# Attention mask added on VectorE, maximum subtracted on GpSimd, later slots for P.V and the value product, feed-forward weights loaded one by one

## The reference, cut to what matters

```python
for i in range(6):                                  # DEPTH
    x = attn_layer(shift_tokens(x), Wqkv[i], q_scale[i], k_scale[i], Wo[i]) + x
    x = ffn_layer(shift_tokens(x), ln_g[i], ln_b[i], W1[i], b1[i], W2[i], b2[i]) + x

# attn_layer: 16 heads of 64, windows of 32 tokens, each looking at itself and the window before
q = rotary(l2norm(q) * qs); k = rotary(l2norm(k) * ksc)
sim = einsum('bhwie,bhwje->bhwij', bq, bk2) * 8.0
sim = where(mask, -finfo.max, sim); attn = softmax(sim, -1)
out = einsum('bhwij,bhwje->bhwie', attn, bv2)  @ Wo
# ffn_layer: layer norm, then (a * gelu(gate)) @ W2 + b2, with a, gate = split(xn @ W1 + b1)
# shift_tokens: the second half of the channels comes from the token before
```

## Time and profile before

| | us |
|---|---|
| three runs: median (lowest to highest) | 1740.41 (1739.14 to 1745.62) |
| the profiled execution | 1741.98 |
| its span, first to last instruction | 1740.2 |
| PE busy | 1666.1 (96%) |
| DVE busy | 1381.5 (79%) |
| POOL busy | 1187.3 (68%) |
| ACT busy | 1092.9 (63%) |
| share of PE in the chain that ended last | 89% |

### The profile page before, as it was taken

One profiled execution on the slowest core, in us unless ns is written; L12 is line 12 of the kernel. 1 busy time (PEld: TensorE's weight loads), 2 busy tenths in 40 slices (PEclk: granted clock), 3 DMA queues, 4 the chain that ended last, 5 costly groups with the idle time before them and its releaser, 6 DMA issues.

```text
span 1740.2 us, 74075 instructions
## 1 busy us (share of the span) xinstructions
PE 1666.1 (96%) x31420; PEld 1210.5 (70%) x31420; DVE 1381.5 (79%) x2661; ACT 1092.9 (63%) x1943; POOL 1187.3 (68%) x1163
## 2 busy tenths in 40 slices
PE   5889999999999999999999999999999999999995
PEld 2357777777777777677777677777677777677774
DVE  4688888887888888788888788888788887788863
ACT  2256666666666666566666566666666666566653
POOL 0377777776777767676776677677677777666751
PEclk9799999999999999999999999999999999999998
DMA  3032223332223323222323222333222332222222
GB/s 106 25 93 66 68 67 79 89 76 71 66 68 81 88 68 78 68 65 69 96 71 78 70 68 63 92 78 77 71 69 66 80 87 74 74 64 66 66 61 76
DMA packets 109735, 127.86 MB, mean 73 GB/s; under 512 B 52064, under 2 KB 55648, under 8 KB 109152
## 3 DMA queue, kind: packets, MB, share of 16 engines
q1 hardware_dynamic: 109408, 123.13, 27.9%
HBM read 20.27 MB, written 2.10 MB: 13 GB/s over the span
## 4 chain that ended last, share of the span: by engine, by line
PE 89%; DVE 4%; SPq 2%; ACT 2%; DMA 2%; issue 1%; POOL 0%; ACTq 0%; DVEq 0%; POOLq 0%
PE QKb L471 21%; PE O L594 11%; PE F L499 9%; PE VTb L512 9%; PE S L471 9%; PE S L529 8%; PE S L559 5%; PE F L616 4%; PE F L628 4%; PE F L629 3%; PE S L522 2%; SPq L397 1%; DVE t L823 1%; PE F L568 1%; DMA prm<-in_params 1%
## 5 line engine op out<-in xcount | busy, mean ns | idle before, releaser
L968 POOL TENSOR_TENSOR t<-t 128x512 f32<-128x512 f32 x384 | 488.7, 1273 | 306.6 <-DVE t L823 298.7
L823 DVE TENSOR_TENSOR t<-QKb,table 128x1024 f32<-128x1024 f32 x384 | 468.8, 1221 | 156.8 <-ACT sq L668 156.3
L962 POOL TENSOR_TENSOR t<-t,rn 128x512 f32<-128x512 f32 x384 | 400.5, 1043 | 136.0 <-DVE rn L863 136.0
L471 PE MATMUL QKb<-wq_sb,x_sh 128*128 128x512 f32 x768 | 426.3, 637 | 12.4 <-DVE t L823 11.7
L668 ACT ACTIVATE sq<-QKb 128x512 f32<-128x512 f32 x384 | 230.8, 601 | 321.7 <-PE QKb L471 314.7
L499 PEld LDWEIGHTS F<-wo_sb,OT 128*128 128x128 f32 x1536 | 202.9, 193 | 89.6 <-issue 88.7
L512 PEld LDWEIGHTS VTb<-cst,t 128*128 128x128 f32 x1536 | 186.6, 141 | 104.8 <-issue 94.0
L512 PE MATMUL VTb<-cst,t 128*128 128x128 f32 x1536 | 230.6, 273 | 0.6 <-POOL t L962 0.5
L594 PEld LDWEIGHTS O<-PT,V 64*64 64x64 f32 x12288 | 199.2, 135 | 42.7 <-issue 41.8
L876 DVE TENSOR_REDUCE ss<-sq 128x16 f32<-128x1024 f32 x192 | 224.4, 1169 | 0.0
L594 PE MATMUL O<-PT,V 64*64 64x32 f32 x12288 | 219.2, 221 | 0.9 <-DVE rn L863 0.5
(11 more groups left out here) (136 smaller groups left out, 2165.9 us busy)
## 6 DMA issues: line engine op xcount, KB each, us to landing
V<-v_tok SPq DMA_DIRECT2D x1440, 64.0 KB, 2.0
wq_sb<-in_wqkv SPq DMA_DIRECT2D x36, 256.0 KB, 3.7
wo_sb<-in_wo SPq DMA_DIRECT2D x6, 512.0 KB, 5.0
xs<-xm SPq DMA_DIRECT2D x48, 64.0 KB
xs<-xm SPq DMA_DIRECT2D x48, 63.5 KB
w_sb<-in_w SPq DMA_DIRECT2D x6, 341.0 KB, 3.3
w_sb<-in_w SPq DMA_DIRECT2D x6, 192.0 KB, 3.1
y_spill<-OT SPq DMA_DIRECT2D x1, 1024.0 KB, 4.1
```

Source lines behind the costliest of these rows:

```text
L471: return pe.matmul(out_, x_sh[:, pr, P * tile:P * (tile + 1)], wq_sb[:, col:col + 512], start=True, stop=True)
L823: dve.tensor_tensor(t12[:, v, :, :].rearrange("p c (h d) -> p c h d", h=8), QK_ps.rearrange("p (h d) -> p h d", h=8).unsqueeze(1) .to_broa ...
L962: pool.tensor_tensor(w, w, rn[:, vv // 4, 8 * (vv % 4):8 * (vv % 4 + 1)].unsqueeze(2) .to_broadcast([P, 8, DH]), ALU.mult).then_inc(qk_nor ...
L968: pool.tensor_tensor(w, w, t12[:, v, 1, :].rearrange("p (h c d) -> p h c d", h=8, c=2)[:, :, ::-1, :], ALU.add).then_inc(add_done, 1)
```

## The change

- **Mask.** The two mask matmuls of each quad go, with `ident_bf` and `mask_bf`. The score matmuls write their banks afresh. DVE adds the mask from `cst` while it moves the scores from `S2` to `E` (semaphore `mask_done`), and takes the maximum from `E`. PE's value projection and PT now wait for `mask_done` where they waited for `sub_done`.
- **Subtraction.** POOL subtracts the maximum, in place in `E`, in a slot of its own (`L_SUB`).
- **Lags.** V from 6 to 8; exponent from 12 to 13, normalisation from 13 to 14, PT from 14 to 16, PV from 16 to 18. In the feed-forward WO from 21 to 22, MID from 24 to 26, SH from 24 to 25, XT from 29 to 33, W1 from 32 to 34, the end from 37 to 38; ST and NM stay at 27. TX goes from slot 6 to slot 7. `Y_BACK`, the slot in which the recurrence's result is transposed back, goes from `STEPS * SLOTS + 19` to `+ 27`.
- **Order in a slot.** All four engines' steps are written in another order. Of the parts named above: PE transposes ahead of the projection; DVE has Newton, END, ST and MID ahead of `t12`; POOL has scale, subtraction, normalisation, NM, and `t12`'s add last.
- **Feed-forward weights.** W1, W2 and the parameters have a semaphore each. W1 is reloaded at slot 36, after the last W1 product of the layer before, W2 at slot 38, and `prm` has two buffers and is loaded at slot 2.

```diff
-L_V = 6
-L_S, L_EXP, L_NORM, L_PT, L_PV = 11, 12, 13, 14, 16
-
-F_WO, F_MID, F_SH, F_ST, F_NM, F_XT, F_AFF = 21, 24, 24, 27, 27, 29, 29
-F_W1, F_GEL, F_HID, F_W2, F_END = 32, 32, 33, 35, 37
-TX = 6
+L_V = 8
+L_S, L_SUB, L_EXP, L_NORM, L_PT, L_PV = 11, 12, 13, 14, 16, 18
+
+F_WO, F_MID, F_SH, F_ST, F_NM, F_XT, F_AFF = 22, 26, 25, 27, 27, 33, 33
+F_W1, F_GEL, F_HID, F_W2, F_END = 34, 34, 35, 37, 38
+TX = 7
...
-                if slot == F_END + 1:
-
-                    wait(sp, ff_final, l * B)
-                    sp.dma_start(w1_sb[:, :], w1[l]).then_inc(in_ffn, 16)
-                    sp.dma_start(w2_sb[:, :, :], w2[l])\
-                      .then_inc(in_ffn, 16)
-                    sp.dma_start(prm[:, :], params[l]).then_inc(in_ffn, 16)
+                if slot == 2:
+
+                    wait(sp, ff_final, (l - 1) * B)
+                    sp.dma_start(prm[:, l % 2, :], params[l]).then_inc(in_prm, 16)
+                if slot == F_HID + 1:
+
+                    wait(sp, w1_ready, l * B * NCH)
+                    sp.dma_start(w1_sb[:, :], w1[l]).then_inc(in_w1, 16)
+                if slot == F_W2 + 1:
+
+                    wait(sp, w2_ready, l * B)
+                    sp.dma_start(w2_sb[:, :, :], w2[l]).then_inc(in_w2, 16)
...
-                        for p in range(2):
-                            pe.matmul(S2[:, p, 0:4 * KEYS], ident_bf[:, :], mask_bf[:, :], start=True, stop=False,
-                                      skip_group_check=True)
...
-                                                   start=False, stop=ct == 3, skip_group_check=True)
...
+                                                   start=True, stop=True)
...
-                        dve.tensor_reduce(mv_, Sv, AX_X, ALU.max).then_inc(max_done, 1)
-                        wait(dve, max_done, a + 1)
-                        wait(dve, pt_ready, a - 3)
-                        if a == 0:
-                            wait(dve, yT_done, 4)
-                        dve.tensor_tensor(E[:, k, :].rearrange("p (c b k) -> p b c k", c=4, b=2), Sv,
-                                          mv_.unsqueeze(3).to_broadcast([P, 2, 4, KEYS]),
-                                          ALU.subtract).then_inc(sub_done, 1)
...
+                    f, pr = batch(s, par, v, F_ST)
+                    if f is not None:
+                        wait(dve, xs_moved, 48 * (f + 1))
...
+                    f, pr = batch(s, par, v, F_MID)
+                    if f is not None:
+                        wait(dve, wo_ready, f + 1)
...
+                        dve.tensor_tensor(Ek, Sv, cst[:, C_MASK:C_MASK + 4 * KEYS]
+                                          .rearrange("p (c k) -> p c k", k=KEYS).unsqueeze(1)
+                                          .to_broadcast([P, 2, 4, KEYS]), ALU.add).then_inc(mask_done, 1)
+                        wait(dve, mask_done, a + 1)
+                        wait(dve, sub_done, a - 3)
+                        dve.tensor_reduce(mx[:, k, :], E[:, k, :].rearrange("p (c k) -> p c k", k=KEYS), AX_X, ALU.max)\
+                           .then_inc(max_done, 1)
...
+                    a, k, st, pr = quad(s, par, v, L_SUB)
+                    if live(a, QUADS):
+                        wait(pool, max_done, a + 1)
+                        w = E[:, k, :].rearrange("p (c k) -> p c k", k=KEYS)
+                        pool.tensor_tensor(w, w, mx[:, k, :].unsqueeze(2).to_broadcast([P, 8, KEYS]),
+                                           ALU.subtract).then_inc(sub_done, 1)
```

More of the change, by code:

```diff
@@ L476, in step @@
                     g = s * SLOTS + v
+                    u, vv, st, pr = unit(s, par, v, L_TR)
+                    if live(u, UNITS):
+                        wait(pe, qk_norm, u + 1)
+                        wait(pe, tr_evac, u)
+                        for i in range(4):
+                            mm = pe.transpose(VT_ps[:, P * i:P * (i + 1)], t12[:, vv, 0, P * i:P * (i + 1)], ident)
+                        mm.then_inc(tr_ready, 1)
                     if live(g, UNITS):
@@ L505, in step @@
-                    recurrence(in_fill(s, v, 0))
-                    u, vv, st, pr = unit(s, par, v, L_TR)
-                    if live(u, UNITS):
-                        wait(pe, qk_norm, u + 1)
-                        wait(pe, tr_evac, u)
-                        for i in range(4):
-                            mm = pe.transpose(VT_ps[:, P * i:P * (i + 1)], t12[:, vv, 0, P * i:P * (i + 1)], ident)
-                        mm.then_inc(tr_ready, 1)
-                    a, k, st, pr = quad(s, par, v, L_S)
@@ new lines, in step @@
+                    a, k, st, pr = quad(s, par, v, L_PT)
+                    if live(a, QUADS):
+                        wait(pe, p_norm, a + 1)
+                        wait(pe, mask_done, s_units(s, v))
+                        wait(pe, pt_evac, a)
+                        for ct in range(4):
+                            mm = pe.transpose(PT_ps[:, P * ct:P * (ct + 1)], E[:, k, P * ct:P * (ct + 1)], ident)
+                        mm.then_inc(pt_ready, 1)
+                    a, k, st, pr = quad(s, par, v, L_S)
@@ L636, in _ @@
         def _(act):
-            act.wait_ge(set_dve, 4)
+            act.wait_ge(set_dve, 2)
             act.wait_ge(mv_done, TILES)
@@ new lines, in step @@
+                    u, vv, st, pr = unit(s, par, v, L_SS)
+                    if live(u, UNITS) and vv % 2 == 0:
+                        wait(dve, sq_done, u + 2)
+                        dve.tensor_reduce(ss[:, vv // 4, 8 * (vv % 4):8 * (vv % 4) + 16],
+                                          sq[:, vv % 4:vv % 4 + 2, :].rearrange("p a (h d) -> p (a h) d", h=8),
+                                          AX_X, ALU.add).then_inc(ss_done, 1)
+                    recurrence(in_fill(s, v, 0))
+                    a, k, st, pr = quad(s, par, v, L_EXP)
@@ new lines, in step @@
+                    if live(a, QUADS):
+                        wait(dve, exp_done, a + 1)
+                        dve.tensor_reduce(sm[:, k, :], E[:, k, :].rearrange("p (c k) -> p c k", k=KEYS), AX_X, ALU.add)\
+                           .then_inc(sum_done, 1)
+                        wait(dve, sum_done, a + 1)
+                        wait(dve, p_norm, a - 3)
+                        dve.reciprocal(rs[:, k, :], sm[:, k, :]).then_inc(rs_done, 1)
+                    recurrence(in_fill(s, v, 1))
```

286 lines of the change are left out of this document (131 added, 155 removed).

## The result

The changed kernel takes **1825.76 us** (median of 4 runs, 1823.79 to 1827.37), the kernel before 1740.86 in the same comparison (4 runs, 1739.14 to 1745.62). The ratio is 1.048, with a 95% interval of 1.046 to 1.051: 85 us slower. The forecast was 1795 with a range of 1744 to 1830, so the sign and the range held, and the loss is 1.6 times the one forecast.

A forecast was written before the change was run, and what follows sets the result against it. PE alone was taken to bound the kernel at 33.35 us per step. Steady steps +37.7, irregular rest +4, clock +10, start +2 and +3, end +3 and -5 gave +54.7 on 1741.98, forecast 1795, range 1744 to 1830.

The forecast's parts named there:

- PE's floor: PE's own work per step without waits on other engines: falls from 33.35 to 32.25 us.
- the floor's two parts: On PE per step: mask matmuls removed save 0.87 us, the new order of matmul groups saves 0.23.
- The boundaries: At layer boundaries PE's wait for the affine step goes with separate weight and parameter loads: 20.7 us saved over five steps.
- MID to ST: Move of shifted rows between MID and the statistics takes 6.3 us, so PE stalls 1.7 per step before Q(4).
- POOL's convoy: NM, waiting for ST, stands ahead of slot 3's add on POOL; PE's slot 6 transposes wait, 0.9 us more per step.
- The step and the clock: Steady step of 34.9 us, 43 steps giving +37.7; PE's clock falling in one step of six or seven, +10 in all.
- The start: First steps: step 3's stall +2 us and the recurrence's DVE additions behind t12 +3.
- The recurrence's places: In the recurrence's first ten slots both its DVE additions stand behind t12: +3 us, range 0 to 6.
- The end: Last batches meet the same wait, +3 us; five mask groups and PE's wait for the recurrence's result go, -5.
- The move is hidden: Rival: the moved rows land before DVE has done the gates, PE keeps its floor; 1670 us, chance 10%.
- Only DVE's wait counts: Rival: POOL catches up and no clock is lost, step 33.95, about 1744 us, no change; chance 12%.
- the clock falls in every step: Rival: each step's stall lowers PE's clock, adding 60 to 80 us, about 1865; chance 8%.

The follow-up runs named there:

- best: st31 with the block of inverse square roots moved behind the maximum, in slots 1 and 5; 1762.82 us, 1.014 of before.
- st29: Changed kernel with layer norm statistics and normalisation two slots later (F_ST = F_NM = 29 instead of 27); 1746.58 us, 1.004 of before.
- before_ff: Kernel before with only the changed kernel's separate loads of W1, W2 and the parameters, old order otherwise; 1720.34 us, 0.990 of before.
- split_rows: Changed kernel with the 127-row transfer cut into 112 and 15 rows, single-row transfer kept; 1718.79 us, 0.987 of before.
- nm31: Changed kernel with only the normalisation's lag moved, F_NM from 27 to 31, statistics left in place; 1793.62 us, 1.030 of before.
- st31: Changed kernel with layer norm statistics and normalisation four slots later (F_ST = F_NM = 31 instead of 27); 1704.85 us, 0.979 of before.
- st31_rec: st31 with the filter's recurrence put back on PE and DVE where the kernel before has it; 1703.08 us, 0.976 of before.
- split_no_row: Changed kernel with the 127-row transfer cut into 112 and 15 rows and the single-row transfer left out; 1704.35 us, 0.979 of before.

## Why the prediction was right in kind, and short in size

**PE's floor, right.** Slots without a wait are seen in the table: 4.70, 3.35, 5.58, 3.10, 3.81, 3.62 (best), 4.70, 3.45. Their sum is 32.3; the forecast was 32.25. The 0.1 between the forecast's 3.35 and the 3.45 of slot 7-0 stands in every kernel of the new order (st29 has 3.80) and is the one part missed. Only the sum of the floor's two parts is shown, 0.87 for the mask and 0.23 for the order: no run parts them in the new order.

**The boundaries, right, with a new item missed.** The wait for the affine step is gone, and before_ff shows the gain alone. But the steps that begin a layer take 36.2 to 38.4 in the changed kernel, not 35.2. Of this 0.68 is in 1-2, which is 4.03 there; the timeline of DVE has the item:

```profile
891.82 1.75 DVE L797 TENSOR_TENSOR table<-cst,scales 128x256 f32<-128x256 f32 x2
```

Two products for the rotary tables stand ahead of slot 0's. The old order absorbed them; the new one has no slack in this place. The rest is mostly in 3-4, which takes 5.2 to 6.2 in these steps: the residual sum ends 1.26 after Q(2) there and not 0.98, so the statistics and all behind them come later by as much. In two of the five steps the clock fell as well (below).

**MID to ST, right and a little small.** The step on which all rested, taking 6.3 from the last batch and not 2.0 from V's rows, held: 6.5. MID ends 0.98 after Q(2), forecast 1.02, and Q(4) came 10.51 after Q(2), where the forecast had 10.34. The reason for the 6.3 wasn't in the forecast; it is the 127 rows. The forecast had quoted the Trainium skill, "DMA: Bandwidth & Descriptors", section "Anatomy of one DMA — SWDGE (gpsimd) path", with a fixed 2.0 us and bytes over bandwidth, and set it aside for the row; that section is on DMAs issued by GpSimd, and these are issued by SP. Its rule fits the large transfers in split_rows, which land after 2.1, and not the 127 rows. The page's rule on the number of engines, which fits what was measured, was not looked at.

**POOL's convoy, right.** 0.9 per step, in the trace of after and by nm31.

**The step and the clock.** A step is 35.23, not 34.9: 0.15 of it in 3-4, 0.05 in 4-5 and 5-6, and 0.1 in 7-0. Over 43 steps that is **+14**. The clock was booked at 10, from an idle 1.58 that was followed by the lower level. PE's idle ahead of Q(4) is about as long as that, 1.42 to 1.63 in 36 of the 43 steps, and behind none of these did the clock fall. It fell to the lower level three times in the 43 steps: behind idles of 1.99 in step 8, 1.96 in step 16 and 2.52 in step 23, and not behind one of 2.02 in step 24. The waits in steps 8 and 24:

```profile
340.13 1.10 PE L475 MATMUL QKb<-wq_sb,x_sh 128*128 128x512 f32 x2 [1.99 <-DVE t L853]
...
909.94 1.10 PE L475 MATMUL QKb<-wq_sb,x_sh 128*128 128x512 f32 x2 [2.02 <-DVE t L853]
```

The windows of the changed kernel (stretch, us, busy us of each engine, granted clock, DMA), in step 8 up to and behind the wait, then a steady stretch:

```profile
335.00:340.00 5.00, 3.14 (x75) 1.80 (x73) 2.04 (x7) 4.00 (x7) 1.65 (x3) 1.00 0.30 73
340.00:350.00 10.00, 9.87 (x151) 6.49 (x152) 7.51 (x17) 4.43 (x8) 8.05 (x8) 0.66 0.35 94
...
1000.00:1100.00 100.00, 93.35 (x1786) 65.73 (x1785) 79.01 (x153) 62.55 (x112) 81.47 (x81) 1.00 0.28 69
```

The three steps with a fall are the longest, 38.4, 36.9 and 36.8, where boundary steps otherwise take 36.3 and other steps 35.2. So the falls cost at most some 4 together (an estimate from these lengths; step 23 has a late DMA issue in it too). So clock and irregular time together were 9 where 14 were booked, and the 43 steps: 51.7 forecast, plus 14, less 5 is the 61.0 measured.

**The start was mis-sized: +13.1, not +5.** The recurrence's places were booked at +3 and are worth 6 (st31 against st31_rec). The stall of step 3 was booked at the steady 2; that step took 36.1 against 30.9, and step 2 another 1.3. In step 3 PE has no W1 product yet (2-3 is 3.81, not 5.58), so it comes to the wait earlier and idles 3.5 in one piece, and the granted clock from 156 to 168 was 0.72: 3-4 takes 7.78.

**The end had the wrong sign: +11.3, not -2.** The last batches' wait was booked at 3. The chain of waits in the tail shows three full landings, with little on PE to cover them:

```profile
1748.81 4.93 DMA xs<-xm
...
1757.25 1.86 PE O L524 x64
...
1776.67 5.16 DMA xs<-xm
...
1797.86 4.84 DMA xs<-xm
```

The attention product takes 1.86 there against 1.06 in the steady steps. The windows behind step 47's first projection, of the changed kernel and of split_no_row (stretch, its length, busy us of each engine with PE's first, granted clock, DMA):

```profile
1704.70:1825.60 120.90, 97.07 (x1801) 76.25 (x1799) 58.80 (x133) 58.33 (x102) 55.02 (x59) 0.86 0.25 65
```

```profile
1598.50:1703.30 104.80, 88.63 (x1800) 69.45 (x1798) 59.20 (x133) 58.06 (x102) 54.92 (x59) 0.95 0.28 75
```

In split_no_row the last four batches wait 2.0 in all for their rows, in the changed kernel 12.5. The kernel before needed 109.6 for this stretch, split_no_row 104.8, so the gain of 5 that the forecast saw at the end was there, and the waits cost 16 where 3 were booked. Of the 16, 8 are time in which PE is idle, and 8 are the same matmuls at a lower clock (97.1 busy against 88.6, granted 0.86 against 0.95). This is the step that failed: the price of a wait was taken from the steady state and carried to a stretch where PE has no other work and where its clock falls with it, and the clock was booked for the steady steps alone.

**The rivals.** "The move is hidden" is what st31 makes of this kernel: 1704.85, not the 1670 priced, since slot 5 (0.5), slot 7-0 (0.1), the start and the tail keep their waits. "Only DVE's wait counts" fell with nm31, "the clock falls in every step" with three falls in 43 steps.

What stays open: why the clock fell behind some of the waits of 2.0 and not behind others, why runs of st31_rec fall in two groups, and whether a place for the inverse square roots exists that neither POOL nor PE feels.

## What to carry to other kernels

A lag in a hand-written pipeline must be checked against the time that the slowest step between its ends takes, transfers included, and that time is read where the trace shows it uncovered, often only in the last batch. When a step is brought forward, list what is queued behind its wait on every engine in order; here 1.8 of the 2.9 us lost per step fell on DVE's next product and 0.9 on POOL's in-order queue. Price the start and the drain of the pipeline apart: a wait that cost 2.9 in a steady step cost some 4 in each of the last four batches (16 together), half of it idle time and half a lower clock.

## What the runs showed of the hardware

A transfer of 127 partitions moved its 63.5 KB at 17 to 20 GB/s, 112 and 15 partitions as two transfers up to 198 GB/s, and that cut alone, which keeps every byte, took the changed kernel from 1825.76 to 1718.79 us. The slow transfer also held up the next issue on SP's queue: 2.73 us instead of 0.57 for a single row, 2.63 instead of 0.59 for 64 KB of V. An idle of 1.42 to 1.63 us once in a step of 35 left PE's granted clock at 1.00; it fell behind three longer ones of 1.96 to 2.52, and not behind one of 2.02. In the tail, at 97 us busy of 121, it was 0.86.
